# Mixture of experts: routing in a table of slots, and the shared expert of two batches beside the reading back of results

## The chip, the core and the metric

One core of a Trainium2 chip runs the whole program in one launch. The metric is the device time of the program in microseconds. The engines are TensorE (PE), VectorE (DVE), ScalarE (ACT) and GpSimd (POOL), each with its own queue of instructions that run in order; SyncE (SP) issues most transfers. Queues meet only by semaphores.

## What is computed

A decoder of two layers on x of 8 batches, 512 tokens and 256 columns: attention, attention to a context, a feed-forward part, and once more with other forms. The last part, the only one that the change touches, is a mixture of 8 experts of which each token takes 2, and a shared expert that all tokens pass through:

```python
xt = x.reshape(-1, H)                                   # H = 256, I = 512, E = 8, TOP_K = 2
shared = jax.nn.silu(xt @ sg_w.T) * (xt @ su_w.T) @ sd_w.T
probs = jax.nn.sigmoid(xt @ router_w.T + routing_bias)
topk_p, topk_idx = jax.lax.top_k(probs, TOP_K)
topk_p = topk_p / jnp.sum(topk_p, axis=-1, keepdims=True)
g = jnp.einsum('th,eih->tei', xt, wg)
u = jnp.einsum('th,eih->tei', xt, wu)
y = jnp.einsum('tei,ehi->teh', jax.nn.silu(g) * u, wd)
routed = jnp.einsum('te,teh->th', w, y)                 # w: topk_p at topk_idx, else 0
return (shared + routed).reshape(orig_shape)            # added to x; x is normalised before
```

## The kernel before

X holds all 8 batches in SBUF, 128 partitions by 4 groups of 256 columns for each batch. Every product is made of three in half precision (high by high, high by low, low by high), so each operand has a high and a low half: the high half is a copy to float16 by ScalarE, the low half the difference. All of the expert phase is in `experts_phase`. Its parts, in order of time:

**Shared stage.** For each batch b of 8, in one loop on each engine written out by hand:
- Routing. VectorE: `norm.statistics`, `apply` (normalised xn; between them GpSimd takes the power in `norm.pool`); ScalarE `high`, VectorE `low` (halves of xn, in xw); TensorE `turn_x` (transposes), ScalarE `high_turned` and VectorE `low_turned` copy the turned halves from PSUM to xt (two buffers, b % 2); TensorE `logits`, VectorE `logits`, ScalarE `sigmoid`, VectorE `choose` (top 2 and their shares), TensorE `ranks`, VectorE `slots` (the slot of each token in its expert's list, slotu), GpSimd 8 indirect writes of rows of xw to the DRAM table xs (L2253).
- Shared expert, in 4 parts i of 128 columns. TensorE `gate_up` (12 products of 512 columns), ScalarE `squash` (silu, L2285, then the high half hh, L2287), VectorE `hidden` (product h, L2415, then the low half hl, L2418). Then TensorE `project` (48 products of 256 columns) and VectorE `update` (added to X, four operations, L2424).
- Weights. SyncE loads the three matrices of the next expert to stage, ScalarE and VectorE split them (`split`, L2266 and L2353, 3 + 3 operations of 1024 columns); nine sets in all, the shared expert's first.

VectorE's order for batch b is statistics(b + 2), hidden(b, 0), hidden(b, 1), slots(b), low_turned(b + 1), hidden(b, 2), hidden(b, 3), logits(b + 1), apply(b + 2), choose(b + 1), low(b + 2), split(b + 1), update(b). After the last batch's slots `tables` works out which block of 128 rows belongs to which expert. SyncE then writes padding rows (L2193, L2197) and waits for it and for all scatters.

**Block loop.** NK = 71 blocks of 128 rows. SyncE reads a block's rows from xs (L2207, NR = 6 buffers); TensorE turns them (`block_turn`), makes gate and up (`block_gate_up`), turns the hidden (`block_turn_hidden`) and projects (`block_down`); ScalarE and VectorE make the halves as above; VectorE scales the result by the token's share (`block_out`) and GpSimd writes it to the DRAM tensor yd by an indirect write (L2258), at the token's number. Buffers: the block's turned rows lie in xt's first buffer, its turned hidden in xt's second; hb and lb are hh and hl.

**End.** When all writes to yd have landed, SyncE reads the first results of each batch (L2213) and ScalarE's queue the second (L2335), token j * 128 + p to partition p, so in pieces of 1 KB; VectorE adds both to X (L2536, L2539); SyncE writes the batch out (L2217).

## Time and profile before

| | us |
|---|---|
| median of 3 runs | 2174.9 (2166.31, 2174.9, 2177.34) |
| profiled execution, its time | 2166.33 |
| profiled execution, its span | 2164.6 |
| TensorE busy | 1685.7 (78%) |
| VectorE busy | 1328.2 (61%) |
| ScalarE busy | 1111.9 (51%) |
| GpSimd busy | 929.9 (43%) |

The span goes from the first instruction to the last one. A granted clock of TensorE of 1.00 is 2.4 GHz, 0.50 is 1.2 GHz. The expert phase begins at 1571.5 us, so it is 593 us of the span. In timelines, a bracket behind an instruction tells how long its engine was idle before it and what released it; "issue" is waiting for nothing that the profile shows. Durations that follow each other on TensorE overlap, as their ends are modelled.

### The profile page before, as it was taken

What the parts mean: (1) busy time and instruction counts of PE and PEld (TensorE: products, weight loads), DVE (VectorE), ACT (ScalarE), POOL (GpSimd) and SP (SyncE); (2) the same over time, 40 slices, a digit from 0 to 9 for tenths busy, and PEclk for the clock granted to TensorE, in tenths of its full rate; (3) what the DMA queues carried; (4) which work ended last, traced back from release to release, by engine and by line L of the source; (5) the groups of instructions that cost most, each with busy time, mean ns of one, the idle gap of its engine ahead of it and who ended that gap; (6) DMA issues with size and microseconds to landing.
All of it is one profiled execution on the core that took longest, in us unless ns stands there. A gap on an engine that the chain in (4) does not pass through costs nothing. (4 is left out here: it accounts for less than half of the span.)

```text
span 2164.6 us, 35976 instructions
## 1 busy us (share of the span) xinstructions
PE 1685.7 (78%) x12334; PEld 860.6 (40%) x12350; DVE 1328.2 (61%) x3655; ACT 1111.9 (51%) x1526; POOL 929.9 (43%) x955
## 2 busy tenths in 40 slices
PE   4888888888687885577777775677658788999992
PEld 2222222222255563233333333344334455666661
DVE  2767777775177995356666663445267774555554
ACT  2367676765365894245555543355344443444440
POOL 3145455531458522367777764345223341222220
PEclk9899999997698998679999977889879999999996
DMA  4342233320130000334333301422123232222217
GB/s 101 64 70 55 56 49 63 57 45 2 43 83 1 1 1 11 62 58 58 57 56 52 51 11 25 95 52 52 26 90 120 103 132 67 61 62 62 61 49 245
DMA packets 120452, 130.26 MB, mean 60 GB/s; under 512 B 21981, under 2 KB 106973, under 8 KB 120125
## 3 DMA queue, kind: packets, MB, share of 16 engines
q1 hardware_dynamic: 109572, 105.54, 24.0%
q0 software_dynamic: 6480, 18.23, 2.2%
q10 hardware_dynamic: 4224, 4.19, 0.6%
q8 instruction: 105, 1.72, 0.3%
q14 instruction: 71, 0.57, 0.1%
HBM read 79.25 MB, written 47.55 MB: 59 GB/s over the span
## 5 line engine op out<-in xcount | busy, mean ns | idle before, releaser
L653 ACT ACTIVATE at_pexp<-ps 128x1024 f32<-128x1024 f32 (+3 forms) x480 | 385.7, 826 | 185.5 <-PE ps L890 184.5
L714 DVE TENSOR_REDUCE at_mx<-ps 128x1 f32<-128x512 f32 x512 | 323.7, 683 | 137.3 <-PE ps L897 135.5
L897 PE MATMUL ps<-at_ks,at_qs 48*128 48x512 f16 (+3 forms) x1024 | 284.5, 353 | 98.4 <-DVE at_mx L714 41.7
L161 PE MATMUL ps<-mo_wall,mo_xt 128*128 x1704 | 301.8, 327 | 0.9 <-issue 0.9
L890 PE MATMUL ps<-at_qs,at_ks 50*128 50x512 f16 (+4 forms) x1024 | 251.8, 345 | 20.5 <-DMA at_qs<-at_mhl 14.5
L950 PE MATMUL ps<-at_pexp,at_vaug 128*32 128x512 f32 (+4 forms) x2048 | 223.1, 528 | 12.0 <-issue 11.8
L161 PEld LDWEIGHTS ps<-mo_wall,mo_xt 128*128 128x128 f16 x1704 | 161.2, 98 | 94.7 <-issue 4.0
L2258 POOL DMA_INDIRECT mo_yd<-mo_xn,mo_idu x71 | 68.2, 960 | 272.1 <-DVE mo_xn L2520 263.0
L716 DVE CUSTOM_DVE_ANT_0 at_junk<-ps,at_lmask 128x192 bf16<-128x192 f32 x384 | 115.6, 352 | 81.8 <-PE ps L897 80.5
L897 PEld LDWEIGHTS ps<-at_ks,at_qs 48*128 48x128 f16 x1024 | 75.8, 97 | 210.5 <-DVE at_mx L714 121.4
L2311 ACT ACTIVATE mo_sg<-ps 128x512 f32<-128x512 f32 x71 | 42.4, 597 | 194.8 <-PE ps L161 194.8
L890 PEld LDWEIGHTS ps<-at_qs,at_ks 50*128 50x128 f16 x1024 | 69.9, 98 | 168.0 <-issue 86.1
L510 POOL TENSOR_TENSOR at_qkl<-at_qk,at_qkh 128x512 f16<-128x512 f32 x68 | 82.7, 1217 | 74.5 <-ACT at_qk L637 71.9
L2509 DVE SCALAR_TENSOR_TENSOR mo_h<-ps,mo_sg 128x512 f32<-128x512 f32 x71 | 49.1, 691 | 104.3 <-ACT mo_sg L2311 104.2
L161 PE MATMUL ps<-mo_xt,mo_sh 128*128 128x512 f16 x384 | 91.6, 395 | 19.1 <-DVE mo_h L2415 10.5
L557 POOL TENSOR_TENSOR at_pexp<-at_pexp,at_keep_l 128x768 int32<-128x768 int32 x48 | 95.1, 1994 | 6.1 <-ACT at_pexp L653 6.1
L2253 POOL DMA_INDIRECT mo_xs<-mo_xw,mo_slotu x64 | 63.5, 993 | 71.3 <-DVE mo_slotu L2410 54.2
L716 DVE CUSTOM_DVE_ANT_0 at_junk<-ps,at_cmask 128x384 bf16<-128x384 f32 (+3 forms) x128 | 57.2, 487 | 52.4 <-PE ps L897 51.2
L950 PEld LDWEIGHTS ps<-at_pexp,at_vaug 128*32 128x32 f32 x2048 | 47.7, 114 | 80.6 <-issue 68.9
L494 POOL TENSOR_SCALAR at_xn<-X,at_mv,at_rstd 128x256 f32<-128x256 f32 x64 | 77.7, 1226 | 1.7
L2514 DVE TENSOR_TENSOR mo_hl<-mo_h,mo_hh 128x512 f16<-128x512 f32 x71 | 49.1, 692 | 44.0 <-ACT mo_hh L2315 44.0
L726 DVE TENSOR_TENSOR at_pexp<-at_pexp,at_keep_f 128x768 f32<-128x768 f32 x48 | 66.0, 1377 | 13.1 <-ACT at_pexp L653 13.1
(399 smaller groups left out, 3754.8 us busy)
## 6 DMA issues: line engine op xcount, KB each, us to landing
at_qs<-at_scratch SPq DMA_DIRECT2D x96, 128.0 KB, 7.1
at_ks<-at_scratch SPq DMA_DIRECT2D x96, 128.0 KB, 7.7
mo_xr<-mo_xs SPq DMA_DIRECT2D x71, 136.0 KB, 2.4
at_scratch<-at_qkh SPq DMA_DIRECT2D x64, 128.0 KB, 1.8
at_scratch<-at_qkl SPq DMA_DIRECT2D x64, 128.0 KB, 1.8
x_qs<-x_queries SPq DMA_DIRECT2D x48, 128.0 KB
mo_stage<-in_m_gate SPq DMA_DIRECT2D x9, 512.0 KB
mo_stage<-in_m_up SPq DMA_DIRECT2D x9, 512.0 KB
```

Of the source, the lines that this page charges most:

```text
L161: last = nc.tensor.matmul(out, lhs, rhs, start=(n == 0), stop=(n == len(terms) - 1))
L494: last = pool.tensor_scalar(norm.xn[:, j, :], r.X[:, at + j * D:at + (j + 1) * D], norm.mv[:, j, 0:1], norm.rstd[:, j:j + 1], ALU.subtract ...
L510: pool.tensor_tensor(qkl[:, m, :], qk32[:, m, :], qkh[:, m, :], ALU.subtract).then_inc(qkl_ready, 1)
L557: pool.tensor_tensor(part.bitcast(I32), part.bitcast(I32), kept, ALU.mult).then_inc(pool_masked, 1)
L653: last = act.activation(columns(pexp[:, U % 2, hh], at, n, stride, width), columns(banks(r, ST[S % 2], 2), at, n, stride, width), ACT.Exp, ...
L714: last = ve.reduce_max(out, score, AX.X)
L716: last = ve.tensor_tensor_reduce(junk[:, i % 3, piece.at:piece.at + piece.n], score, piece.mask[:, 0:piece.n], 1.0, NEG, ALU.add, ALU.max, ...
L726: ve.tensor_tensor(part, part, keep_f[:, P:].rearrange("p (s w) -> p s w", w=LW), ALU.min).then_inc(vector_masked, 1)
L890: return nc.tensor.matmul(banks(r, ST[(b * K + k) % 2], 2)[:, piece.at:piece.at + piece.n], ks[rows, b % 2, h // 2, piece.idx * P:(piece.i ...
L897: return nc.tensor.matmul(banks(r, MX[i % 2])[:, piece.at:piece.at + piece.n], qs[rows, (n // 2) % 2, h // 2, piece.idx * P:(piece.idx + 1 ...
L950: last = nc.tensor.matmul(banks(r, O)[32 * hh:32 * hh + 32, piece.lo:piece.lo + piece.n], vaug[:, b % 2, piece.idx, h, :], pexp[:, (b * NU ...
L2258: pool.indirect_dma_start(yd[:], bass.IndirectOffsetOnAxis(ap=idu[:, k % 8:k % 8 + 1], axis=0), yt[:, k % 4, :], None).then_inc(y_out[k % ...
```

## The change

Only `experts_phase` is changed.
- Two tables of slots and a third for the weights (ROUTE with period 28, SHARED with 42, SPLIT with 35) give each step of each batch a slot; on every engine one loop over the slots t issues what is due, in a fixed order within a slot. Routing of all 8 batches is in the table, the shared expert of six (FIRST = 6).
- xt has four buffers, for batches b % 4. Both turned halves are copied by ScalarE (`x_turned`). The low half of the hidden is made by GpSimd (`low_hidden`), and `hidden` waits for it two parts back before it writes h again. ScalarE's silu and its high half are steps of their own (`squash`, `high_hidden`). `update` and `project` work by half batches, one operation of 512 columns in place of two of 256. Each of the three weight matrices is loaded and waited for by itself. GpSimd issues its 8 scatters at slots of their own.
- project(5) and update(5) come behind the first block's gate and up. gate_up(6, 0) stands ahead of the hidden's transposes of the last block, gate_up(6, 1) ahead of the last `block_down`.
- The rest of batches 6 and 7 (HELD) comes behind the block loop, on all engines; on VectorE its products h stand between the additions of batches 0 to 5.
- Row buffers lie in xw, which scatters have left by then, and are 8 in place of 6; onehot lies in ge. Tokens are numbered p * 4 + j, so a partition's four rows lie together in yd; both results are read on SyncE's queue, 4 KB a partition, and the output is written by half batches.

```diff
-NR = 6
+NR = 8
 EW = 2 * 3 * NW
+
+
+ROUTE = {"STAT": -22, "RSTD": -17, "APPLY": -10, "HIGH": -10, "LOW": 2, "TURN": (-9, 6), "XT": (-3, 12), "LG": 6, "LOGITS": 17, "SIG": 16,
+         "CHOOSE": 20, "RANK": 18, "SLOTS": 27, "SCAT": (28, 30, 33, 49, 49, 49, 50, 51)}
+ROUTE_PERIOD = 28
+SHARED = {"GU": (11, 12, 41, 45), "SQ": (22, 33, 48, 50), "H": (26, 42, 49, 56), "HH": (38, 47, 48, 62), "HL": (43, 50, 66, 70), "PROJ": (64, 66),
+          "UPD": (77, 97)}
+SHARED_PERIOD = 42
+SPLIT = {"LOAD": (-105, -83, -71), "WHI": (-58, -42, -34), "WLO": (-42, -28, -19)}
+SPLIT_PERIOD = 35
+FIRST = 6
...
+        def due(t, kind):
+
+            at, K, n = tables_of[kind]
+            return [(b, i) for i, offset in enumerate(at) for b, rest in (divmod(t - offset, K),) if rest == 0 and 0 <= b < n]
...
+            for t in range(START, END):
+                for s, n in due(t, "LOAD"):
+                    load_weights(s, n)
...
-                sp.dma_start(yb[:, b, 0, :].rearrange("p (j c) -> p j c", c=D),
-                             yd[b * T:(b + 1) * T].rearrange("(j p) c -> p j c", p=P)).then_inc(y0_in[b], 16)
+                for k, arrived in enumerate((y0_in, y1_in)):
+                    sp.dma_start(yb[:, b, k, :], yd[(k * B + b) * T:(k * B + b + 1) * T].rearrange("(p j) c -> p (j c)", j=NJ)).then_inc(arrived[b], 16)
...
+            def scatter(b, i):
+                if i == 0:
+                    pool.wait_ge(slot_ready, b + 1)
+                    pool.wait_ge(lo_ready, b + 1)
+                pool.indirect_dma_start(xs[:], bass.IndirectOffsetOnAxis(ap=slotu[:, b, i:i + 1], axis=0),
+                                        rows(b % 3)[:, i % NJ, :], None).then_inc(scattered[b % 3], 16)
+
+            def low_hidden(b, i):
+                n = b * NI + i
+                pool.wait_ge(hh_ready, n + 1)
+                pool.tensor_tensor(hl[:, i, :], h[:, pair(n), :], hh[:, i, :], ALU.subtract).then_inc(hl_ready, 1)
+
+            for t in range(START, END):
+                for b, _ in due(t, "RSTD"):
+                    norm.pool(pool, b)
+                for b, i in due(t, "HL"):
+                    low_hidden(b, i)
+                for b, i in due(t, "SCAT"):
+                    scatter(b, i)
...
+            for b in HELD:
+                for i in range(NI):
+                    low_hidden(b, i)
...
+            def x_turned(b, p):
+                act.wait_ge(turned, 2 * b + p + 1)
+                if b >= 4:
+                    act.wait_ge(gu_done, NI * (b - 3))
+                act.activation(xt[:, b % 4, p], half_bank(p), ACT.Copy).then_inc(xt_ready, 1)
...
+            def high_hidden(b, i):
+                n = b * NI + i
                 act.wait_ge(h_ready, n + 1)
-                act.activation(hh[:, i, :], h[:, i % 2, :], ACT.Copy).then_inc(hh_ready, 1)
+                if b in HELD:
+                    act.wait_ge(ht_done, NK)
+                if b:
+                    act.wait_ge(dn_done, 2 * b)
+                act.activation(hh[:, i, :], h[:, pair(n), :], ACT.Copy).then_inc(hh_ready, 1)
...
+                if n >= 2 and n - FIRST * NI not in (0, 1):
+                    ve.wait_ge(hl_ready, n - 1)
+                ve.scalar_tensor_tensor(out=h[:, pair(n), :], in0=banks(r, GU[pair(n)][1]), scalar=1.0 / WS, in1=sg[:, pair(n), :],
                                         op0=ALU.mult, op1=ALU.mult).then_inc(h_ready, 1)
-                ve.wait_ge(hh_ready, n + 1)
-                ve.tensor_tensor(hl[:, i, :], h[:, i % 2, :], hh[:, i, :], ALU.subtract).then_inc(hl_ready, 1)
-
-            def update(b):
-                ve.wait_ge(dn_done, b + 1)
-                for j in range(NJ):
-                    x = r.X[:, b * BT + j * D:b * BT + (j + 1) * D]
-                    last = ve.scalar_tensor_tensor(out=x, in0=banks(r, DN, 2)[:, j * D:(j + 1) * D], scalar=1.0 / WS, in1=x,
-                                                   op0=ALU.mult, op1=ALU.add)
-                last.then_inc(x_done, 1)
+
+            def half_x(b, half):
+                return r.X[:, b * BT + half * 2 * D:b * BT + (half + 1) * 2 * D]
+
+            def update(b, half):
+                ve.wait_ge(dn_done, 2 * b + half + 1)
+                return ve.scalar_tensor_tensor(out=half_x(b, half), in0=banks(r, DN + half), scalar=1.0 / WS, in1=half_x(b, half), op0=ALU.mult, op1=ALU.add)
...
+            for t in range(START, END):
+                for b, i in due(t, "H"):
+                    hidden(b, i)
+                for b, _ in due(t, "LOGITS"):
+                    logits(b)
+                for b, _ in due(t, "CHOOSE"):
+                    choose(b)
+                for b, _ in due(t, "SLOTS"):
+                    slots(b)
+                if t == TABLES:
                     tables()
-                split(b + 1)
-                update(b)
+                for b, _ in due(t, "LOW"):
+                    low(b)
+                for b, _ in due(t, "APPLY"):
+                    apply(b)
+                for b, _ in due(t, "STAT"):
+                    norm.statistics(ve, r, b)
+                for b, half in due(t, "UPD"):
+                    if b < FIRST - 1:
+                        update(b, half).then_inc(x_done, 1)
+                for s, n in due(t, "WLO"):
+                    split(s, n)
...
+            early, late = HELD
+            hidden(early, 0)
+            hidden(early, 1)
+            add(0)
+            hidden(early, 2)
+            add(1)
+            hidden(early, 3)
+            add(2)
+            hidden(late, 0)
+            add(3)
+            hidden(late, 1)
+            add(4)
+            hidden(late, 2)
+            add(5)
+            add(early)
+            finish(early)
+            hidden(late, 3)
+            add(late)
+            finish(late)
...
+            for t in range(START, END):
+                for b, p in due(t, "TURN"):
+                    turn_x(b, p)
+                for b, _ in due(t, "LG"):
+                    logits(b)
+                for b, _ in due(t, "RANK"):
+                    ranks(b)
+                for b, i in due(t, "GU"):
+                    gate_up(b, i)
+                for b, half in due(t, "PROJ"):
+                    if b < FIRST - 1:
+                        project(b, half)
...
             block_gate_up(0, bases[0])
+            for half in range(2):
+                project(FIRST - 1, half)
             for k in range(NK):
                 if k + 2 < NK:
                     block_turn(k + 2)
                 if k + 1 < NK:
                     bases.append(weight_base(k + 1))
                     block_gate_up(k + 1, bases[k + 1])
+                else:
+                    gate_up(FIRST, 0)
                 block_turn_hidden(k)
                 if k:
                     block_down(k - 1, bases[k - 1])
+            gate_up(FIRST, 1)
             block_down(NK - 1, bases[NK - 1])
+            gate_up(FIRST, 2)
+            gate_up(FIRST, 3)
+            for b in HELD:
+                if b > FIRST:
+                    gate_up(b, 0)
+                    for half in range(2):
+                        project(b - 1, half)
+                    for i in range(1, NI):
+                        gate_up(b, i)
+            for half in range(2):
+                project(nb - 1, half)
```

## Rows read from the trace of the kernel before

**Rows 1.** Windows by stage: length, busy us (x instructions) per engine, PE clock, DMA share, GB/s.

```profile
1571.50:1594.10 22.60, 2.83 (x40) 2.27 (x40) 15.54 (x60) 8.99 (x10) 4.59 (x19) 0.50 0.21 71
1594.10:1773.90 179.80, 147.92 (x1034) 88.08 (x1035) 128.37 (x423) 88.93 (x116) 61.04 (x62) 0.91 0.33 115
1773.90:1795.06 21.16, 9.74 (x64) 6.67 (x62) 14.35 (x36) 4.70 (x6) 8.70 (x8) 0.77 0.37 127
1795.06:1806.90 11.84, 11.35 (x61) 5.40 (x62) 4.50 (x15) 3.52 (x6) 0.00 (x0) 0.83 0.26 71
1806.90:2112.60 305.70, 305.70 (x2407) 201.77 (x2405) 166.26 (x469) 135.79 (x201) 63.80 (x67) 1.00 0.21 58
2112.60:2126.90 14.30, 9.75 (x85) 6.97 (x83) 4.76 (x10) 5.08 (x7) 4.36 (x5) 0.99 0.14 47
2126.90:2164.60 37.70, 0.00 (x0) 0.00 (x0) 19.60 (x16) 0.00 (x0) 0.00 (x0) 0.50 1.02 334
```

**Rows 2.** Waits, 1571 to 1800 us: total us, times, longest.

```profile
POOL mo_xs L2253 <- DVE mo_slotu L2410: 54.2, 8, 13.0
```

**Rows 3.** Chain of work that ended last, 1590 to 1800 us: start, us, what.

```profile
1691.93 3.40 DVE mo_wall L2353 x3
```

**Rows 4.** Groups of VectorE, 1571 to 1791 us: count, busy us, mean ns, idle before.

```profile
L2353 DVE SCALAR_TENSOR_TENSOR mo_wall<-mo_stage,mo_wall 128x1024 f16<-128x1024 f32 x24 | 27.9, 1215 | 0.0
...
L2418 DVE TENSOR_TENSOR mo_hl<-mo_h,mo_hh 128x512 f16<-128x512 f32 x32 | 22.2, 692 | 22.3 <-ACT mo_hh L2287 20.9 <-issue 1.4
...
L2415 DVE SCALAR_TENSOR_TENSOR mo_h<-ps,mo_sg 128x512 f32<-128x512 f32 x32 | 22.0, 687 | 9.7 <-ACT mo_sg L2285 9.6
...
L2424 DVE SCALAR_TENSOR_TENSOR X<-ps,X 128x256 f32<-128x256 f32 x32 | 11.2, 411 | 0.0
...
L2365 DVE COPY mo_xt<-ps 128x1024 f16<-128x1024 f16 x8 | 5.5, 690 | 3.3 <-PE ps L2559 3.3
```

**Rows 5.** Groups and lines of GpSimd: scatter, subtraction in attention (min/median/max), power of the norm.

```profile
L2253 POOL DMA_INDIRECT mo_xs<-mo_xw,mo_slotu x64 | 63.5, 993 | 71.3 <-DVE mo_slotu L2410 54.2 <-issue 17.1
...
L510 POOL TENSOR_TENSOR at_qkl<-at_qk,at_qkh x68: 1152/1155/1876, 20.3 to 1317.7; 128x512 f16<-128x512 f32 x68
...
L155 POOL TENSOR_TENSOR mo_rstd<-mo_var,mo_power x8: 1008/1040/1044, 1577.3 to 1724.0; 128x4 f32<-128x4 f32 x8
```

**Rows 6.** Timeline from the last slots to the first block: start, us, operation.

```profile
1773.73 0.17 DVE L2410 CAST mo_slotu<-mo_slotf 128x8 uint32<-128x8 f32 x1
...
1778.05 0.16 DVE L2429 TENSOR_TENSOR mo_cnt<-mo_base,mo_ebase 128x8 f32<-128x8 f32 x1
...
1790.63 39.47 SPq L2207 DMA_DIRECT2D mo_xr<-mo_xs  x15
...
1795.06 4.68 PE L161 MATMUL ps<-mo_wall,mo_xt 128*128 x12 [0.40 <-issue]
```

**Rows 7.** Timeline of TensorE: gate/up of the first batch, cold and warm.

```profile
1594.13 7.04 PE L161 MATMUL ps<-mo_xt,mo_sh 128*128 128x512 f16 x24 [8.60 <-DVE mo_sh L2353]
...
1605.07 2.75 PE L161 MATMUL ps<-mo_xt,mo_sh 128*128 128x512 f16 x12
```

**Rows 8.** Timeline of the end: first reading, additions of batch 0.

```profile
2126.89 12.88 SPq L2213 DMA_DIRECT2D mo_wall<-mo_yd  x8
...
2131.91 1.23 DVE L2536 TENSOR_TENSOR X<-X,mo_wall 128x1024 f32<-128x1024 f32 x1 [8.33 <-DMA mo_wall<-mo_yd]
...
2133.24 1.22 DVE L2539 TENSOR_TENSOR X<-X,mo_wall 128x1024 f32<-128x1024 f32 x1
```

**Rows 9.** Windows of transfers: weights (2 KB packets), results read, output written.

```profile
1575.00:1576.00 1.00, 0.00 (x0) 0.00 (x0) 0.84 (x3) 0.00 (x0) 0.00 (x0) 0.50 1.06 377
...
2140.00:2150.00 10.00, 0.00 (x0) 0.00 (x0) 7.92 (x7) 0.00 (x0) 0.00 (x0) 0.50 1.10 348
...
2158.00:2162.00 4.00, 0.00 (x0) 0.00 (x0) 0.00 (x0) 0.00 (x0) 0.00 (x0) 0.50 1.09 385
```

**Rows 10.** Window of the first attention stage, whose order comes from a slot table.

```profile
250.00:500.00 250.00, 216.23 (x1452) 65.17 (x1456) 189.48 (x342) 174.19 (x200) 118.25 (x137) 0.98 0.32 53
```

249 lines of the change are left out of this document (106 added, 143 removed).

## The prediction

> **What bounds the kernel now.** I read the table of slices first, to find where no engine is full, then the windows by stage, the waits and the chain, and last the timelines at the seams. In the windows [rows 1] the reader is to see five pieces of the expert phase, which is the only part that the change touches. A head of 22.6 us, in which TensorE does 2.8 us. A shared stage of 179.8 us up to the last slots (end of the cast of slotu, 1773.9), in which TensorE is busy for 147.9 us (82%) and VectorE for 128.4 (71%), so neither is full. A seam of 21.2 us to the first routed block. The block loop, where TensorE is busy for 305.7 of 305.7 us at clock 1.00. And an end of 37.7 us, in which TensorE and ScalarE do nothing and the transfers run all the time, at a mean of 334 GB/s.
>
> GpSimd waited 54 us for slots in all [rows 2]: it is not the bound today. The chain in the shared stage changes its engine all the time; a piece that returns for each batch is the three weight splits on VectorE, 3.40 us in a row [rows 3], which stand in the program between one batch's routing and the next batch's hidden parts. So the stage is set by the order in which four queues meet, not by one engine's work. That can be reordered. The block loop can't: there TensorE is full, and what is put into it costs its own length.
>
> **Part 1, the shared stage.** The change writes the order out in a table of slots: routing of a batch every 28 slots, its shared expert every 42, a weight split every 35. It also takes work off VectorE. I count what VectorE executes up to the end of slots(7). Before: 15.54 + 128.37 = 143.9 us [rows 1]. Of this go: 30 low halves of the hidden, now GpSimd's, 30 x 0.692 = 20.8; 8 copies of the turned low half, now ScalarE's, 8 x 0.690 = 5.5; 11 of 30 products h (the table has 19 of them before slots(7), since two batches are held and the shared expert lags), 11 x 0.687 = 7.6; one of 24 splits, 1.2; 28 additions of 0.411 become 7 of twice the width, priced as the product h of the same width: 11.5 - 7 x 0.687 = 6.7 [rows 4]. Left: 143.9 - 41.8 = 102.1 us of VectorE.
>
> It starts later than today (1575.2), since a split now stands ahead of the first statistics: the weights flow from 1575 on at 377 GB/s [rows 9], the first half megabyte is there by about 1576, ScalarE's half takes about 1 us, so 1577. How full can VectorE be? Today 71%. In an attention stage of this kernel whose order comes from such a table it is at 189.5/250 = 76%, with TensorE, the fullest engine there, at 216.2/250 = 86% [rows 10]. I take 76%, as the same engine in the same kind of order: 102.1/0.76 = 134 us, so slots(7) end at 1711. The ends: 71% gives 1721, 86% gives 1696.
>
> GpSimd must keep up. Up to slots(7) it has 56 scatters at (63.5 + 17.1)/64 = 1.26 us with their issue, 70.6 us, 18 subtractions of 1.155, 20.8 us, and 6 powers of 1.04, 6.2 us [rows 5]: 97.6 us. It can begin at the first slots, today at 1605, and by my count of the new head some 5 us earlier, at 1600: floor 1698, so below VectorE's 1711 but near. If each subtraction cost the maximum seen, 1.876, the floor would be 1711. TensorE up to there has 20 gate/up groups and 4 projections. A group of 12 took 2.75 us [rows 7]; a projection, 48 products of half the width, twice that, 5.5. This is 55 + 22 = 77 us, plus some 2 us a batch for turning, logits and ranks, 93 in all from about 1590: it isn't the bound. ScalarE was busy for 88.9 us in the stage [rows 1] and gains 5 us or so by the copies: neither.
> Term 1: 1773.9 to 1711, **-62.6 us**, ends -78 and -53.
>
> GpSimd's price has a rule against it. In the attention stage this very subtraction costs GpSimd 1.155 us where VectorE takes 0.692, a ratio of 1.67 [rows 4, 5]. The Trainium skill, GPSIMD Engine Reference, section 4.1 (Engine selection), says not to use GpSimd for a two-input elementwise operation, as it is about 2 times slower; by that the 18 would take 4 us more, which the trace does not bear out. The sum goes by the trace.
>
> **Part 2, the seam.** From the end of slots(7) to the first block's product it takes 21.2 us today: the table starts 4.2 us after the slots, 12.6 us later the first row read is issued (eight padding writes and the scatters come ahead of it), 4.4 us later TensorE starts [rows 6]. In the new order one product h stands between slots and tables, so 1.5 us instead of 4.2; the eight scatters, 10.1 us, with one subtraction between, end at about +12 and land about +14, where the padding ends too (1.5 + 12.6). Gain 2.7 us; VectorE has four splits, four products and two additions between the tables and the first block_in, some 9 us, to about +17, which just fits. **-2 us**, ends -4 and +4 (these run late).
>
> **Part 3, into the block loop.** project(5) is moved behind the first block's gate/up: 48 products. The 12 of full width follow each other in 2.6 us or so when warm, so 48 of half width are 5.1 us; TensorE has 0.5 us of gaps there to fill (the fourth window) [rows 1]. **+4.6**, ends +4 and +6. gate_up(6,0) and (6,1) stand ahead of the last two block_downs: 24 products, 5.1 us, in gaps of about 0.7 us in the last block: **+4.4**, ends +3 and +5.1. Both delay all behind them.
>
> **Part 4, the end.** The reading moves to one queue and, since tokens are numbered by partition, four rows of a partition lie together: 4 KB instead of 1 KB. Beside it run the shared expert's last six gate/up groups and two projections, 15.4 + 10.2 us of TensorE. From the first read's issue to the last instruction is 37.7 us [rows 1]. Two paths can set it.
> The transfers: 8.4 MB read at 348 GB/s is 24.1 us, 4.2 MB written at 385 is 10.9 [rows 9], and 1.5 us to start: 36.5. If the reads ran like the 2 KB packets of the weights, 377, they would take 22.3 us, 34.7 in all.
> VectorE: batch 0 lies ready 5.0 us after the issue today and takes 2.55 us to add [rows 8]; with one queue in the order y0, y1 the first half lies there after about 3.3. Then up to the last hidden: 7 additions of 2.55, six products of 0.69, two updates of 0.69: 3.3 + 17.9 + 4.1 + 1.4 = 26.7. Behind it, one after another: ScalarE's copy 0.7, GpSimd's subtraction 1.2, projection 5.1, update 0.7, write and landing 2.7: 37.1. TensorE will have stood idle for some 10 us before that projection. After such idle time 24 products took 7.04 us at the start of the stage, where warm ones take 2 x 2.6 [rows 7]: the lower clock (0.50 of full, 1.2 GHz, in the first window of [rows 1], against 1.00, 2.4 GHz, in the loop) costs 1.8 us. So 38.9, plus 0.3 behind the last write. The second path wins: **+2 us**, ends -3 (transfers set it) and +10 (VectorE waits for held parts as well).
>
> On the packets the row shows 348 GB/s at 1 KB and 377 at 2 KB. The Trainium skill, DMA: Bandwidth & Descriptors, section Specifications, has line rate from 512 B on and a limit of about 358 GB/s for memory traffic of a core; by it the larger packets bring nothing and the reads stay at 24 us. The 377 speaks against the limit, not for the packets. Neither changes the sum, whose last term VectorE sets.
>
> **The sum.** -62.6 - 2 + 4.6 + 4.4 + 2 = -53.6 us. The profiled run took 2166.3 us (span 2164.6): 2112.7. The median of the three is 2174.9, 8.6 above; a new median may fall near either, and I add half: **2117 us**.
>
> **The rivals.**
> *It packs better* (14%): the queues meet as in the table, VectorE reaches 86%, and the transfers set the end: -78 - 2 + 4.6 + 4.4 - 2 = -73, 2093 to 2100. For it: TensorE reaches this share in [rows 10]. Against: GpSimd's floor of 1698 leaves nearly nothing.
> *The end grows* (15%): the products h stand between additions, and each waits for ScalarE's silu and, two parts back, for GpSimd's subtraction. If every one of the six holds VectorE for 1.5 us and the projection is cold, the end is 10 to 12 us longer: -53.6 + 9 gives 2122 on the run's time, 2126 with the half. With VectorE at 71% on top, 2136.
> *Slower, GpSimd as the lock* (5%): the new wait in hidden(), on hl_ready two parts back, puts VectorE behind GpSimd, where up to four scatters (5.0 us) are queued ahead of the subtraction; behind the waiting VectorE stand choose and slots, for which the scatters wait. If the two never overlapped, a batch of 28 slots would cost VectorE's 134/8 = 16.8 and GpSimd's 97.6/8 = 12.2 us one after the other, 29 us: 1577 + 8 x 29 = 1809, +35, with the other terms +44: 2210. It decides from slots(7) at 1765 on, 23.5 us a batch. Against it: the table leaves 2 to 14 slots between a subtraction and the product that waits for it, and 54 us of GpSimd's idle time are there to use.
> *It does not do what it says* (4%): the stage stays TensorE's, whose share is the highest today; only the two held batches (31 us of TensorE) leave it, 9 of them come back in the loop and the rest of the slack is used up by waits: within 0.5% of now to -20 us.
> The forecast has 62%, from 2102 to 2134.
>
> **How the numbers follow.** The range takes the forecast's own span, the better packing to the middle of its case and the longer end: 2098 to 2142. What is left out is the rest of the first rival, the last two, and half of what lies above 2136: under 2 in 10. About 0.5% is what a measurement of this kernel can tell from no change. Faster by more: 0.92; within: 0.03; slower: 0.05.
>
> **What the profile would show.** Part 1 right: the last cast of slotu ends 110 to 145 us after the first split, VectorE at 74 to 80% between; wrong: GpSimd without gaps from the first scatter to the last (it is the bound), or VectorE waiting for GpSimd's hl. Part 2: 17 to 22 us from that cast to the first block's product; if the wait there is for VectorE, the splits ran late. Part 3: the loop from first product to last block_down longer by 8 to 10 us. Part 4: from the first read's issue to the end 36 to 41 us; if the last hidden's product starts earlier than 24 us after the issue, transfers set it. Most wrong would be an occupancy of VectorE outside 71 to 86%: one point there is 1.8 us.

## The result, and the profile after

The kernel before took 2174.2 us (median; 2166.3 to 2177.3), the changed one 2148.9 (2145.0 to 2149.8): a ratio of 0.987, 95% interval 0.984 to 0.991. The profiled execution has a span of 2142.9 us (2164.6 before). That is 25 us less where the prediction had 57 (2174.2 to 2117), and outside its range of 2098 to 2142. The direction was right, the size was not.

The windows of the changed kernel, cut at the same marks as [rows 1] (columns as there). The rows are the head to the first gate/up, the stage to the last cast of slotu, the seam to the first block's product, the loop in two pieces (its first 11.8 us, and the rest), and the end from the first reading's issue. From here on "the stage" means head and stage together.

```profile
1575.00:1595.10 20.10, 2.73 (x41) 2.24 (x42) 12.83 (x32) 10.08 (x11) 6.06 (x19) 0.50 0.61 184
1595.10:1726.80 131.70, 102.95 (x768) 59.63 (x766) 112.62 (x380) 82.27 (x103) 94.90 (x81) 0.86 0.41 132
1726.80:1755.30 28.50, 16.73 (x95) 9.67 (x93) 18.99 (x37) 7.10 (x11) 16.27 (x14) 0.81 0.43 136
1755.30:1767.10 11.80, 11.79 (x76) 7.56 (x77) 2.71 (x7) 1.23 (x2) 0.00 (x0) 0.88 0.30 82
1767.10:2095.80 328.70, 326.99 (x2559) 214.84 (x2558) 175.29 (x491) 145.43 (x215) 69.53 (x73) 1.00 0.20 56
2095.80:2142.90 47.10, 28.34 (x157) 16.61 (x155) 29.02 (x26) 7.15 (x12) 9.24 (x7) 0.86 0.72 268
```

Set beside [rows 1], the expert phase is 567.9 us where it was 593.1:

| part | before | after | forecast | measured |
|---|---|---|---|---|
| phase start to last slots | 202.4 | 151.8 | -62.6 | -50.6 |
| seam | 21.2 | 28.5 | -2 | +7.3 |
| loop | 331.8 | 340.5 | +9.0 | +8.7 |
| end | 37.7 | 47.1 | +2 | +9.4 |
| sum | 593.1 | 567.9 | -53.6 | -25.2 |

I compare phases, not spans: the code ahead of the phase is the same in all kernels here, yet the phase began anywhere from 1571.5 to 1588.0 us in their traces.

VectorE in the stage was to be busy for 102.1 us; here it is 12.83 + 112.62 = 125.4. Its groups up to the last slots (line, operation, out<-in, count | busy us, mean ns | idle before) say where the 23 us are; the rows that answer to [rows 4] stand among them.

```profile
L2401 DVE SCALAR_TENSOR_TENSOR mo_wall<-mo_stage,mo_wall 128x1024 f16<-128x1024 f32 x20 | 25.2, 1266 | 0.0
L141 DVE TENSOR_SCALAR mo_xn<-X,mo_mv,mo_rstd 128x256 f32<-128x256 f32 x32 | 14.2, 505 | 1.8 <-POOL mo_rstd L155 1.8
L2463 DVE SCALAR_TENSOR_TENSOR mo_h<-ps,mo_sg 128x512 f32<-128x512 f32 x19 | 13.0, 685 | 2.1 <-ACT mo_sg L2331 1.5 <-issue 0.6
L123 DVE BATCH_NORM_STATS2 mo_stats<-X 128x6 f32<-128x256 f32 x32 | 11.2, 411 | 0.0
...
L131 DVE TENSOR_SCALAR mo_var<-mo_mv 128x4 f32<-128x4 f32 x8 | 7.0, 871 | 0.3
L2471 DVE SCALAR_TENSOR_TENSOR X<-ps,X 128x512 f32<-128x512 f32 x8 | 5.5, 684 | 2.4 <-issue 1.6 <-PE ps L161 0.8
L2433 DVE TENSOR_TENSOR mo_oh<-mo_iota,mo_idxf 128x32 f32<-128x32 f32 x16 | 5.0, 356 | 0.0
...
L2442 DVE TENSOR_TENSOR mo_xw<-mo_pick 128x32 f32<-128x32 f32 x8 | 4.3, 539 | 0.3
```

The kernel before has mo_var at 170 ns, mo_oh at 183, mo_xw<-mo_pick at 192, mo_xn at 408; the splits and the low half of x stood at 1215 to 1219 and are at 1266 and 1339. What did not move is the product h, which reads PSUM (687, now 685), and the statistics (410, now 411). Count times difference of means, over all groups up to the last slots: 20.3 us. I call this held time: the operation is recorded as running, but for longer than its work takes.

Which instances are long shows in the timeline (start, us, engine, operation): an operation of 32 or of 8 columns takes 1.6 or 1.8 us instead of 0.2, and ends less than 0.1 us after a subtraction of GpSimd beside it.

```profile
1666.71 1.62 DVE L2436 TENSOR_TENSOR mo_member<-mo_oh 128x32 bf16<-128x32 f32 x1
1667.10 1.17 POOL L2288 TENSOR_TENSOR mo_hl<-mo_h,mo_hh 128x512 f16<-128x512 f32 x1
...
1721.12 1.83 DVE L2430 SCALAR_TENSOR_TENSOR mo_share<-mo_top,mo_rec 128x8 f32<-128x8 f32 x1
1721.74 1.17 POOL L2288 TENSOR_TENSOR mo_hl<-mo_h,mo_hh 128x512 f16<-128x512 f32 x1
```

GpSimd pays in the other direction: its power (L155) took 1.614 us in the mean for 1.040 in [rows 5]. But the waits (answering to [rows 2]) say that it was not the bound in the stage: it still waited for slots.

```profile
POOL mo_xs L2282 <- DVE mo_slotu L2456: 22.9, 8, 7.8
...
ACT mo_wall L2310 <- DMA mo_stage<-in_m_down: 10.9, 1, 10.9
```

The second row is the seam: ScalarE waited 10.9 us, once, for a weight matrix. From the timeline behind the tables:

```profile
1730.67 3.05 DVE L2491 TENSOR_TENSOR mo_xn<-mo_xw,mo_blocks 128x568 f32<-128x568 f32 x1
...
1736.43 1.20 DVE L2401 SCALAR_TENSOR_TENSOR mo_wall<-mo_stage,mo_wall 128x1024 f16<-128x1024 f32 x1
...
1737.66 0.37 SPq L2214 DMA_DIRECT2D mo_stage<-in_m_down  x1
...
1739.90 8.62 SPq L2228 DMA_DIRECT2D mo_xs<-mo_padt  x8
...
1750.72 21.23 SPq L2238 DMA_DIRECT2D mo_xw<-mo_xs  x12
```

SyncE's queue holds the load of the last expert's third matrix ahead of the eight padding writes and the first row read. The load waits for the split that frees its buffer, and this split stands behind the tables on VectorE. So the eight padding writes begin at 1739.9, 13.1 us after the slots, and the first row is asked for at +23.9. In the kernel before they began at +5.9 and the first row was asked for at +16.7 [rows 6]; my count had the padding start with the tables. The first row of the fence is one of the operations of the tables: beside two subtractions in a row it took 3.05 us, where the kernel before has 0.74, so 2.3 us of the delay are held time again.

The end (answering to [rows 8]), additions and the last two hidden parts:

```profile
2117.31 0.69 DVE L2463 SCALAR_TENSOR_TENSOR mo_h<-ps,mo_sg 128x512 f32<-128x512 f32 x1 [4.55 <-ACT mo_sg L2331]
...
2118.74 1.41 POOL L2288 TENSOR_TENSOR mo_hl<-mo_h,mo_hh 128x512 f16<-128x512 f32 x1 [2.71 <-ACT mo_hh L2340]
2119.26 1.97 DVE L2579 TENSOR_TENSOR X<-X,mo_wall 128x1024 f32<-128x1024 f32 x1
...
2128.76 0.68 DVE L2463 SCALAR_TENSOR_TENSOR mo_h<-ps,mo_sg 128x512 f32<-128x512 f32 x1
...
2131.64 0.40 PE L161 MATMUL ps<-mo_sh,mo_hh 128*128 128x256 f16 x1 [9.82 <-POOL mo_hl L2288]
```

VectorE waits 4.55 us for a silu whose gate/up stands behind project(6) on TensorE; the additions beside a subtraction take 1.96 to 1.99 us for 1.23 (four of them ahead of the last product h, one behind it); the last product h starts 33.0 us after the first issue (by my sum 26.7 less 0.7 for itself, 26.0); and TensorE stands idle for 9.8 us before the last projection, which runs from 2131.64 to 2139.6. The transfers are not what it waits for: they read faster than in [rows 9], 1 KB packets at 348 GB/s, now 4 KB:

```profile
2100.00:2104.00 4.00, 1.33 (x4) 0.57 (x5) 3.73 (x5) 1.12 (x2) 0.64 (x1) 0.85 1.02 416
2104.00:2108.00 4.00, 3.12 (x10) 0.96 (x7) 3.87 (x4) 1.23 (x2) 1.57 (x2) 0.72 1.03 411
```

### The profile page after: what moved, and what is told of

Read it like the earlier page. It is cut to its first block and busy times, and to the rows that moved or that the text cites. A ratio compares the mean times of both kernels' runs of the same rounds, so it can differ in the third digit from the quotient of the medians.

```text
span 2142.9 us, 36053 instructions
## 1 busy us (share of the span) xinstructions
PE 1689.5 (79%) x12334; PEld 861.9 (40%) x12350; DVE 1323.9 (62%) x3599; ACT 1119.2 (52%) x1534; POOL 982.8 (46%) x987
## 5 line engine op out<-in xcount | busy, mean ns | idle before, releaser
L714 DVE TENSOR_REDUCE at_mx<-ps 128x1 f32<-128x512 f32 x512 | 323.9, 685 | 137.1 <-PE ps L897 135.3
L890 PE MATMUL ps<-at_qs,at_ks 50*128 50x512 f16 (+4 forms) x1024 | 251.0, 343 | 20.8 <-DMA at_qs<-at_mhl 15.9
L161 PE MATMUL ps<-mo_xt,mo_sh 128*128 128x512 f16 x384 | 97.0, 413 | 9.8 <-DVE mo_h L2463 9.8
L2282 POOL DMA_INDIRECT mo_xs<-mo_xw,mo_slotu x64 | 72.1, 1126 | 38.2 <-DVE mo_slotu L2456 22.9
L527 POOL TENSOR_SCALAR at_m<-at_mx 128x32 f32<-128x32 f32 x32 | 9.5, 297 | 140.5 <-DVE at_mx L714 122.1
```

The source lines that it names most:

```text
L161: last = nc.tensor.matmul(out, lhs, rhs, start=(n == 0), stop=(n == len(terms) - 1))
L714: last = ve.reduce_max(out, score, AX.X)
L890: return nc.tensor.matmul(banks(r, ST[(b * K + k) % 2], 2)[:, piece.at:piece.at + piece.n], ks[rows, b % 2, h // 2, piece.idx * P:(piece.i ...
L2282: pool.indirect_dma_start(xs[:], bass.IndirectOffsetOnAxis(ap=slotu[:, b, i:i + 1], axis=0), rows(b % 3)[:, i % NJ, :], None).then_inc(sca ...
```

## The experiments

Theory: GpSimd's subtractions hold operations of VectorE, the small ones above all, wherever both engines run, so part 1's move of work is worth nothing; the seam is SyncE's queue behind the tables; the end is the order of VectorE's queue. Rival: the table packs badly, whatever engine subtracts, and transfers set seam and end. The stage, seam and end lengths below are cut at the marks of the table above. The diffs are shortened: "..." and lines with # stand for what is left out.

### The subtraction back on VectorE (e1)

```diff
 # GpSimd
-                for b, i in due(t, "HL"):
-                    low_hidden(b, i)
 # VectorE
             for t in range(START, END):
+                for b, i in due(t, "HL"):
+                    low_hidden(b, i)
                 for b, i in due(t, "H"):
```

> The 24 low halves of the hidden of the shared stage go back from GpSimd to VectorE, in the same slots of the table; everything else as after. Held-operand theory (VectorE's operations with two inputs in SBUF, or the short ones around the power, are held until GpSimd's running operation ends; this made 23 us of VectorE's 125 us of busy time up to the last slots): VectorE gains 24 x 0.69 = 16.6 us of work and loses most of the 23 us of holding, so its busy time up to slots(7) stays within 118 to 127 us, the means of the small two-input operations (0.36 to 0.54 us in after) fall back to 0.18 to 0.25, the stage stays within 4 us of after, the program 2140 to 2153. If the scatters and not the subtractions hold it, the means stay as in after and the stage grows by 15 us or so: 2160 to 2166. Queue theory (GpSimd's queue is what sets the stage, not VectorE's held time): freed of 30 us, it lets the stage shorten by 8 us or more: below 2141.

Measured: the stage 145.3 us instead of 151.8, the program 2140.2 us (0.986 of before, 0.982 to 0.990). The window of its stage:

```profile
1574.10:1719.40 145.30, 101.74 (x804) 59.91 (x804) 115.95 (x429) 92.27 (x113) 77.13 (x81) 0.85 0.44 145
```

VectorE now does 18 more subtractions in that stretch, 12.3 us at 682 ns each, and is busy for 9.5 us less (115.95 for 125.4); the one-hot compare is back at 183 ns, mo_var at 219. GpSimd's help was a loss of 6.5 us. That is more than the expectation allowed (busy 118 to 127, a stage within 4 us), and the program's 2140.2 lies just below the 2141 that it gave to the other theory, a GpSimd queue that sets the stage. What decides between them is VectorE's idle time: a freed queue would have shortened its waits, but it went from 26.4 us (151.8 - 125.4) to 29.4 (145.3 - 115.95). The gain is all in busy time.

### One part alone, on the kernel before (e10)

```diff
 # VectorE, hidden()
+                if n >= 2:
+                    ve.wait_ge(hl_ready, n - 1)
-                ve.wait_ge(hh_ready, n + 1)
-                ve.tensor_tensor(hl[:, i, :], h[:, i % 2, :], hh[:, i, :], ALU.subtract).then_inc(hl_ready, 1)
 # GpSimd: the same subtraction, parts 0 and 1 ahead of a batch's scatters, 2 and 3 among them
```

> The kernel before with one part of the change alone: the 32 low halves of the hidden on GpSimd, two ahead of a batch's scatters and two among them; the order of everything else stays. Theory of the held operand: VectorE loses 22 us of subtractions, but gets back 10 to 20 us by its small two-input operations lying beside GpSimd's, and each hidden part reaches TensorE later (1.25 us for 0.69, or more behind a scatter): the stage is not shorter, -2 to +12 us against the kernel before on the same chip, and the groups of the normalization and of the one-hot products on VectorE show means raised as in the changed kernel. Rival, that work taken from VectorE is worth its length at its occupancy of 71% as my prediction counted: the stage is 20 to 29 us shorter and the small operations are as short as before.

Measured beside the kernel before on the same chip (e12, below): the stage 213.8 us against 200.6, the program 2190.4 against 2174.0 us. The window, and four groups of VectorE up to 1800 us:

```profile
1583.80:1797.60 213.80, 149.09 (x1068) 91.35 (x1069) 144.48 (x451) 97.42 (x125) 102.17 (x111) 0.81 0.30 104
```

```profile
L2427 DVE SCALAR_TENSOR_TENSOR mo_h<-ps,mo_sg 128x512 f32<-128x512 f32 x31 | 21.4, 692 | 34.9 <-ACT mo_sg L2295 31.0 <-POOL mo_hl L2251 3.8
...
L2434 DVE SCALAR_TENSOR_TENSOR X<-ps,X 128x256 f32<-128x256 f32 x28 | 9.9, 417 | 17.1 <-PE ps L161 17.1
...
L2397 DVE TENSOR_TENSOR mo_oh<-mo_iota,mo_idxf 128x32 f32<-128x32 f32 x16 | 10.5, 697 | 0.0
...
L2420 DVE CAST mo_slotu<-mo_slotf 128x8 uint32<-128x8 f32 x8 | 8.2, 1027 | 0.3
```

30 subtractions of 0.692, 20.8 us, left VectorE, and it is busy for 144.5 us against 144.35: the one-hot compare went from 183 to 697 ns, the cast of the slots from 171 to 1027, and all such differences together are 19.5 us. So VectorE's work did not get shorter, and its waits got longer by the 13 us of the stage: 72.9 us of idle time ahead of all its groups, where e12 has 59.9. The product h now waits 34.8 us there, as long as product and subtraction waited together before (9.6 and 20.9) and 4 us more; new are the 17.1 us for the projection ahead of `update`, which comes later because its low halves do. Smaller waits went away. The 13.2 us are just above the expected +12; the rival's -20 to -29 us is refuted; this one edit, by itself, makes the kernel 0.9% slower than before (0.6 to 1.2).

### What holds what (e6)

A probe behind the end of the kernel before (semaphores left out of the diff): VectorE repeats five kinds of operation, first alone, then beside 11 subtractions of GpSimd, then beside 12 indirect writes.

```diff
+            for phase in range(3):
+                for _ in range(4):
+                    ve.tensor_tensor(probe[:, n, :], sg[:, 0, :], h[:, 0, :], ALU.add)
+                    ve.scalar_tensor_tensor(out=probe[:, n + 1, :], in0=banks(r, 2), scalar=1.0, in1=sg[:, 1, :], ...)
+                    ve.tensor_scalar(probe[:, n + 2, :], sg[:, 0, :], 2.0, None, ALU.mult)
+                    ve.tensor_reduce(lg[:, 0, 0:1], sg[:, 1, :], AX.X, ALU.add)
+                for c in range(8):
+                    ve.tensor_tensor(small[:, phase, c, 0:16], sg[:, 0, 0:16], h[:, 0, 0:16], ALU.add)
```

> The kernel before, with a probe behind its last addition, which adds time: VectorE runs three times the same row of operations (512 columns in float32: a sum of two operands in SBUF, a product of a PSUM and an SBUF operand, a one-input product in SBUF, a reduction of one operand; then eight sums of 16 columns), first alone, then beside 11 of GpSimd's two-input subtractions, then beside 12 indirect writes. Held-operand theory: beside the subtractions the two-input sums grow from about 0.69 and 0.17 us to up to 1.8 us each, the PSUM product and the reduction stay within 5%; beside indirect writes they grow less than by a fifth. Rival (all of VectorE slows beside GpSimd, a matter of bandwidth): all four forms grow by a like share.

The timeline: the last round alone, the last beside subtractions, and the small sums beside the indirect writes.

```profile
2149.93 0.69 DVE L2556 TENSOR_TENSOR mo_wall<-mo_sg,mo_h 128x512 f32<-128x512 f32 x1
2150.54 0.68 DVE L2557 SCALAR_TENSOR_TENSOR mo_wall<-ps,mo_sg 128x512 f32<-128x512 f32 x1
2151.14 0.42 DVE L2558 TENSOR_SCALAR mo_wall<-mo_sg 128x512 f32<-128x512 f32 x1
2151.47 0.68 DVE L2559 TENSOR_REDUCE mo_lg<-mo_sg 128x1 f32<-128x512 f32 x1
2152.19 0.77 DVE L2563 TENSOR_TENSOR mo_wall<-mo_sg,mo_h 128x16 f32<-128x16 f32 x8
2153.11 16.17 POOL L2265 TENSOR_TENSOR mo_wall<-mo_sg,mo_h 128x512 f32<-128x512 f32 x11 [40.34 <-DVEq L2554]
...
2161.98 1.04 DVE L2556 TENSOR_TENSOR mo_wall<-mo_sg,mo_h 128x512 f32<-128x512 f32 x1
2162.95 0.68 DVE L2557 SCALAR_TENSOR_TENSOR mo_wall<-ps,mo_sg 128x512 f32<-128x512 f32 x1
2163.55 0.88 DVE L2558 TENSOR_SCALAR mo_wall<-mo_sg 128x512 f32<-128x512 f32 x1
2164.35 0.67 DVE L2559 TENSOR_REDUCE mo_lg<-mo_sg 128x1 f32<-128x512 f32 x1
2165.06 4.33 DVE L2563 TENSOR_TENSOR mo_wall<-mo_sg,mo_h 128x16 f32<-128x16 f32 x8
...
2178.82 0.77 DVE L2563 TENSOR_TENSOR mo_wall<-mo_sg,mo_h 128x16 f32<-128x16 f32 x8
```

Beside a subtraction the sum of two SBUF operands goes from 0.69 to 1.04 us, the one-operand multiplication from 0.42 to 0.88, and eight sums of 16 columns from 0.77 to 4.33; the product with one operand in PSUM and the reduction keep 0.68 and 0.67. GpSimd pays too: 16.17/11 = 1.47 us each for 1.155 [rows 5]. Its indirect writes leave the small sums at 0.77 and the large ones at 0.69; the multiplication took 0.57 and 0.54 us in two of its four rounds beside them, which the expectation of two-input operations alone had not foreseen. So it is the subtraction, not the scatters (that of the kernel before ran beside VectorE all the time, and its means are the short ones). The Trainium skill, SBUF — State Buffer, section "SBUF: two separate sides", has this as a rule: GpSimd and VectorE share a pair of ports, and whichever starts first, GpSimd's operation or a VectorE operation with two SBUF inputs or in a two-port mode, has them for the whole instruction. The probe agrees in the sums, which are held, and in the product and the reduction, which are not; the multiplication agrees if it runs in such a mode, which no row here names. Which of the two started first the rows do not bear out: the operation at 1666.71 in the timeline above was held though its record starts 0.39 us ahead of the subtraction's. I had not weighed the rule.

### The tables three slots later (e2)

```diff
-        TABLES = ROUTE["SLOTS"] + ROUTE_PERIOD * (nb - 1) + 1
+        TABLES = ROUTE["SLOTS"] + ROUTE_PERIOD * (nb - 1) + 4
```

> The block tables come three slots later than in after, behind the last but three of the weight splits (7,2) in place of ahead of it. Theory (the seam grew because SyncE stands at the load of the last expert's third matrix, which waits for split(7,2) behind the tables, and the padding writes stand behind that load in SyncE's queue): the load is issued some 8 us earlier, padding follows at once, the first rows are read 7 to 8 us earlier, the seam from the last cast of slotu to the first block's product falls from 28.6 to 20 to 22 us, the program by 6 to 8 us. Rival (the seam is set by VectorE's leftover of splits, products and additions, or by the scatters): no change beyond 2 us.

Measured: stage 151.6, seam 22.0 instead of 28.5, phase 558.7, program 2138.4 us (0.985, 0.981 to 0.988); the seam lies at the upper edge of the expected 20 to 22. The split now stands ahead of the tables, and SyncE comes to the padding early:

```profile
1729.72 1.21 DVE L2401 SCALAR_TENSOR_TENSOR mo_wall<-mo_stage,mo_wall 128x1024 f16<-128x1024 f32 x1
1730.96 0.37 SPq L2214 DMA_DIRECT2D mo_stage<-in_m_down  x1
...
1733.78 3.02 SPq L2228 DMA_DIRECT2D mo_xs<-mo_padt  x3
```

A load that waited behind a table cost 6.5 us; transfers did not.

### The end in another order (e3), and both (e4)

```diff
             hidden(late, 0)
             add(3)
+            add(4)
+            finish(early, x_done)
             hidden(late, 1)
-            add(4)
+            add(5)
             hidden(late, 2)
-            add(5)
+            ve.wait_ge(x_done, 2 * early + 2)
             add(early)
-            finish(early)
             hidden(late, 3)
             add(late)
-            finish(late)
+            settle()
+            finish(late, sum_ready)
 # TensorE: project waits for x_done alone
```

> Only the end's order on VectorE is changed: the addition of batch 4 and the update of batch 6 stand ahead of the product h(7,1), and h(7,3) ahead of the additions of batch 7 but no longer behind the update of batch 6, which now goes ahead of its own additions; project(7) waits for that update alone. Theory (the end is set by VectorE's order: 4.6 us of waiting for silu(7,1) behind project(6), and the last product h late, not by transfers): h(7,3) starts 3 to 5 us earlier, the end from the first read's issue falls from 47.1 to 41 to 44 us, the program by 3 to 6 us. Rival (transfers set the end): no change, since nothing of them is changed.

> e2 and e3 together. They lie in different stages, so the gains add if both theories hold: 9 to 14 us below after, 2135 to 2140. If the earlier start of the block loop only moves its wait elsewhere, less than the sum.

Measured: with e3 the end is 42.3 us instead of 47.1 (program 2143.9 us); with both, seam 21.9 and end 42.4, the phase 555.1 (program 2140.6 us, 0.984, 0.979 to 0.988; expected were 2135 to 2140). The two faults are separate and add up in the phase: 567.9 - 6.6 - 4.7 = 556.6. In the new order TensorE still stands idle before the last projection, 6.0 us instead of 9.8.

### The shared expert of the held batches taken out (e8), and the wide reads alone (e7)

e8 is the changed kernel without the shared expert of batches 6 and 7 (their gate/up, products and projections are left out of the result). e7 is the kernel before with tokens numbered by partition, so that both reads of results move 4 KB at a time; its two queues stay. Both ran on a second chip, as e5 and e6 did; the block loop of e7 took 331.9 us there, as before (331.8), so the loops can be compared.

```diff
 # e8, TensorE
-            gate_up(FIRST, 1)
             block_down(NK - 1, bases[NK - 1])
-            gate_up(FIRST, 2)
...
 # e7, the first of the two readings; the second and the numbers of the tokens likewise
-                sp.dma_start(yb[:, b, 0, :].rearrange("p (j c) -> p j c", c=D),
-                             yd[b * T:(b + 1) * T].rearrange("(j p) c -> p j c", p=P)).then_inc(y0_in[b], 16)
+                sp.dma_start(yb[:, b, 0, :], yd[b * T:(b + 1) * T].rearrange("(p j) c -> p (j c)", j=NJ)).then_inc(y0_in[b], 16)
```

> After, with the shared expert of batches 6 and 7 left out (their output lacks it). It shows what the two held batches cost where they lie now. By my terms: the loop 8.7 us shorter (332 us), the end down to what reading, adding and writing need, 20.4 + 10.9 + 2 = 33 to 35 us in place of 47.1, so 12 to 14 us of the end are theirs, not 2 as predicted. Rival (the end's length is in the transfers, slowed by the work beside them): the end stays above 42 us.

> The kernel before with one part of the change alone: tokens numbered by partition, so that the results are read in 4 KB pieces, still on two queues. In after the windows of the reading show 410 to 424 GB/s. If the packet size does that: the end from the first read's issue falls from 37.7 to 33 to 34.5 us, the program by 3 to 4.5 us. If it came from the single queue: no change.

The windows of their ends, e8 and then e7:

```profile
2098.40:2132.40 34.00, 0.00 (x0) 0.00 (x0) 19.42 (x16) 0.00 (x0) 0.00 (x0) 0.51 0.98 370
```

```profile
2121.90:2156.10 34.20, 0.00 (x0) 0.00 (x0) 19.50 (x16) 0.00 (x0) 0.00 (x0) 0.50 0.98 368
```

The reads alone take the end from 37.7 to 34.2 us; as a program e7 is level with before (0.998, 0.996 to 1.000), as 3.5 us are 0.16%. On the changed kernel the held batches cost 47.1 - 34.0 = 13.1 us in the end, and 340.5 - 336.3 = 4.2 in the loop. The expected loop of 332 us was a miss of its own making: e8 leaves project(5) behind the first block, and 336.3 - 331.8 = 4.5 is what that costs. So the work "beside the reading" is not hidden: two batches, 1/4 of the shared expert, come to 17.3 us where they were held.

### All three edits (e5): a miss

> e1, e2 and e3 in one kernel. The expert phase (from the first load of the router's weights to the end) was 567.9 us in after, 560.9 in e1, 558.7 in e2, 565.2 in e3, 555.1 in e2 + e3. If the stage's gain by e1 (6.5 us, held operations) is independent of the seam and the end: 547 to 550 us, the program 2128 to 2134. If in e1 the gain came from a slack that e2 uses too (VectorE's leftover ahead of the first block), 553 to 556 us: no better than e4.

Edits e1, e2 and e3 together. The stage was 143.7 and the end 42.4, but the seam 28.8 again: phase 556.3, program 2141.6 us on another chip, on which the kernel before took 2162.4 (0.990, 0.987 to 0.992). The padding was not late this time. Its timeline:

```profile
1739.08 0.67 DVE L2512 TENSOR_TENSOR mo_hl<-mo_h,mo_hh 128x512 f16<-128x512 f32 x1
...
1741.20 0.39 PE L161 MATMUL ps<-mo_sh,mo_hh 128*128 128x256 f16 x1 [6.74 <-DVE mo_hl L2512]
...
1749.23 5.34 PE L161 MATMUL ps<-mo_xt,mo_sh 128*128 128x512 f16 x24
...
1754.41 0.39 PE L2699 MATMUL ps<-mo_ident,mo_xw 128*128 128x128 f16 x4
```

The low halves, VectorE's again, now stood behind the tables; project(4) waited 6.7 us for one, and the first block's rows, asked for at 1746.7 (+16.3), had to wait for TensorE until 1754.4. Then TensorE waited 3.35 us more for VectorE's copy of the turned rows (at 1757.6); ahead of it stood, among others, two low halves of 1.48 us together.

### Low halves on VectorE only where nothing waits behind the tables (e9)

```diff
 # e4, and in the two loops over the table
                 for b, i in due(t, "HL"):      (GpSimd)
-                    low_hidden(b, i)
+                    if b >= 4:
+                        low_hidden(b, i)
+                for b, i in due(t, "HL"):      (VectorE)
+                    if b < 4:
+                        low_hidden(b, i)
```

> The changed kernel with the tables three slots later and the end reordered, and with the low halves of the hidden back on VectorE for batches 0 to 3 only; GpSimd keeps them for batches 4 to 7. Theory: the stage gains about as in the kernel with all low halves on VectorE (145.3 against 151.8 us), since only the last part of it still has GpSimd's subtractions: 144 to 148. The seam stays at about 22 us, because no low half stands behind the tables on VectorE any more, where it cost 28.8. The end 42.4. Phase 549 to 554 us, against 555.1 for the two edits without the move. Rival, that the long seam of the three edits together comes of something else than the low halves behind the tables: the seam is 27 to 29 and the phase 555 to 558.

Measured: stage 146.9, seam 22.2, end 43.4, phase 551.6 us, the shortest of all. As a program it took 2140.5 us (0.984, 0.981 to 0.988) against 2146.5 (0.990, 0.987 to 0.993) for the changed kernel on the same chip. The phase is 16.3 us shorter, the program 6: in this trace the code ahead of the phase took 12.9 us longer, with a granted clock of 0.80 for 0.92 in the first 200 us. Why is not settled; no run here separates e2, e4 and e9 as programs.

### Both kernels again on one chip (e11, e12)

> The changed kernel as it is, beside the others on one chip. Theory: its stage is 151 to 153 us as in every run so far of kernels with its stage, and the phase about 568. The gain against the kernel before depends on that kernel's stage, which was 202.4 us in one run and 188.9 in two runs on another chip: 23 to 28 us where the kernel before takes the longer, 10 to 15 where it takes the shorter one.

> The kernel before once more, for its stage on the chip of these runs. Two theories of why it took 202.4 us in one trace and 188.9 in two others, with VectorE busy for 144 us in all of them: either the chip or execution decides it, then this run shows one of the two lengths, the longer with a granted clock that falls to 0.86 in the stage; or the two kernels with 188.9 owe it to their own edit (both differ from the kernel before at the end of the program), then this run shows 202 whatever the chip.

Measured: the changed kernel has stage 151.8, seam 28.3, loop 340.6, end 47.2 once more (2146.5 us); the kernel before has a stage of 200.6 (2174.0 us). The stage of the kernel before in e12:

```profile
1578.60:1779.20 200.60, 148.06 (x1074) 88.84 (x1075) 144.35 (x482) 97.92 (x126) 65.62 (x81) 0.88 0.32 111
```

e6 and e7, whose stages are unchanged, took 188.9 us with VectorE busy for the same 144 us. e12 by itself fits both of its theories. For the first, that the chip or execution decides, speaks that e6 and e7 ran on the chip on which the kernel before itself took 2162.4 us, 10 to 14 less than on the other; but no unedited kernel was traced there, and what makes a batch of the old order take 22.5 or 25 us stays open. The changed kernel's stage is between 151.6 and 152.5 in all six traces that have it, on both chips. So the gain depends on where one measures: 25 us of phase here, and, if the stages of e6 and e7 stand for the kernel before, about 12 less on the other chip.

## Why the prediction was wrong, step by step

**What bounds the kernel: right, but not what the order alone gives.** No engine was full in the stage. Of the 50.6 us that it lost, much is less work: VectorE's own work up to the last slots fell from 143.9 to 105.1 us (held time taken off), by 27%, and the stage by 25%. What the order gives shows in e1: 19% less work (115.95 us), a stage 28% shorter. No run has the new order with all eight batches in it, so the shares of the table and of the two held batches are not shown.

**Part 1, the count of VectorE's work: the step that failed.** "It also takes work off VectorE", 143.9 - 41.8 = 102.1 us, took the durations of [rows 4] as fixed. They were means beside a GpSimd that only scattered. With the subtraction on GpSimd, 20.3 us came back as held operations; 125.4 - 20.3 = 105.1, so the count of the work itself was right to 3 us. GpSimd was priced at its own time only, with "must keep up" as its single condition. Costs were looked for in whom its slowness would hold up; the cost lay in its running at all. The price that I weighed against it, a subtraction 2 times slower than VectorE's, was the harmless one: it took 1.249 us in the stage for 0.692.

**Part 1, the occupancy: not one number.** The 76% was meant from the first split on. Measured there: 125.27 of 145.5 us, 86%, with held time counted as busy, and 72% without (105.1). The signs that the prediction set, 110 to 145 us and "74 to 80% between", misled: 86% is the share of its rival that packs better, and was high because operations waited inside themselves. In e1, with nearly nothing held, it is 115.6 of 139.0 us, 83%, so there 76% was too low: by the same sum e1 would have taken (102.1 + 18 x 0.692)/0.76 = 150.7 us. The attention window of [rows 10] was a poor neighbour for it: 171.8 of VectorE's 189.5 us there are one reduction that reads PSUM (L714), a form that the probe shows not to be held. The lower end, 71%, gave slots at 1721; they came at 1726.8, which is 1723.3 counted from a phase that starts at 1571.5. Of the 12.0 us that the term missed, e1 gives back 6.5; how the other 5.5 divide is open.

**Part 2: wrong, by the step that has the tables start 1.5 us after the slots and the padding end 12.6 us later.** The tables did start early (at +1.0); what was overlooked is that SyncE reaches the padding only past the weight load, and that this load hangs on a split which the early tables push back. Moving the tables ahead moved them past the work that released SyncE. Held time inside the tables added 2.3 us (3.05 for 0.74). With the tables later (e2) the seam is 22.0 for the 19.2 forecast, inside its end of +4.

**Part 3: right.** +4.5 for project(5) and +4.2 for the two gate/ups, against +4.6 and +4.4. Where TensorE is full, counting its instructions is enough.

**Part 4: the right path, mis-sized.** VectorE and the last projection set the end, transfers did not. The sum had 39.2 us (37.1 + 1.8 + 0.3; put down as +2 on 37.7), measured are 47.1. The last product h came 7.0 us later than summed (33.0 for 26.0): VectorE idled 4.55 us for the silu behind project(6), which the sum had at nothing, and four additions beside subtractions took 0.74 us more each, 3.0; 0.5 us were saved elsewhere. Behind that product it took 0.9 us more, mostly the projection, 8.0 for 6.9. The rival "the end grows" named waits for silu and came near in size, 10 to 12 us where +9.4 were measured, but by six waits of 1.5 us; there was one, of 4.55, and the held additions stand in no rival. So its size is in part luck. The larger pieces, worth nothing in the sum, took 3.5 us off the end by themselves (e7: 34.2 us, where the prediction had 34.7 for faster reads).

**The chances.** The forecast's 62% lay on a range that knew one uncertainty, occupancy. The nearest rows for the moved operation were those of the attention stage's subtraction, and I read its own duration from them, not its neighbours'. The trace of the kernel before could have warned: in a later attention stage one multiplication of VectorE with two SBUF operands (L726, at_pexp, 128x768) lasts from 0.944 to 2.407 us over its 48 instances, and the long ones looked at lie beside GpSimd's two-input operations, such as 2.40 us at 1098.86 beside two that take 4.29 us together. The subtraction's own long instances, 1.86 to 1.88 us like the maximum in [rows 5], lie beside this multiplication.

## What to carry to other kernels

When work is moved to a helper engine, price its neighbours as well: look in the trace for operations whose longest instance is far above their shortest without a wait, and see what the helper did then; a part run alone (e10) would have shown the loss in one run. Where a step is moved ahead in one queue, follow each release that it now delays into the other queues (a load behind a split behind a table) to the first transfer that the next stage needs. Work put beside a transfer is hidden only if its own chain, last part included, ends before the transfer does: here it did not, by 13 us.

## What the hardware showed that I had not expected

A VectorE operation of 32 columns can last up to 2.96 us (mo_xw<-mo_pick at 1651.60, else 0.192) beside two of GpSimd's subtractions in a row (2.28 us), in a record where it waits for nothing; this one instance makes the mean of 539 ns above. Its repeat e11 has none like it (192 ns) and 2.8 us less of busy time, with the same stage of 151.8 us, so not all held time lengthens the stage. Results were read at 411 to 416 GB/s in 4 KB pieces against 348 in 1 KB pieces, and in e7 at 411 to 419 with the two queues of the kernel before, so it is the size of the pieces, not the single queue. And the same kernel's shared stage ran at 200.6 to 202.4 us in two traces, and at 188.9 in two others whose edits lie elsewhere.
